# Three edits on three stages of a layered attention kernel: folded up-projections, one inversion for all causal sums, paired last chunks of a down product

## The reference

```python
# first stage, x after layernorm
q = (x @ Wq.T);  kv_latent = x @ Wkv_down.T           # 8 heads x 64; rank 64
k = kv_latent @ Wk_up.T;  v = kv_latent @ Wv_up.T      # 8 heads x 64
attn = softmax(q k^T * HEAD_DIM ** (-0.5));  x = x + (attn v) @ Wo.T
# feed-forward part of each of the four middle layers
a, g = split((layernorm(shift_token(x)) * lg + lb) @ w1 + b1)   # 682 each
x = x + (a * gelu(g)) @ w2 + b2
# causal stage, per head of 16
scores = dot * dot / (q_norm_sq + k_norm_sq.T - 2.0 * dot + EPSILON)   # masked above the diagonal
x = x + (softmax(scores) v) @ w_out + b_out
```

## Time and profile before

| | |
|---|---|
| median of 3 runs | 4794.3 us (4789.01 to 4796.3) |
| the profiled execution | 4790.7 us, span 4788.8 us |
| busy share of the span | PE 89%, PE weight loads 54%, DVE 70%, ACT 54%, POOL 33% |
| granted TensorE clock, mean | 0.947 |
| DMA | 77.63 MB, mean 16 GB/s |

### The profile page before, as it was taken

How to read it: one execution, slowest core, us unless ns; L and a number is a source line. 1 busy time by engine, 2 the same in 40 slices (tenths; PEclk the granted TensorE clock), 3 DMA queues, 4 the chain that set the end, 5 groups by cost and what they waited for, 6 DMA issues and landing times.

```text
span 4788.8 us, 65343 instructions
## 1 busy us (share of the span) xinstructions
PE 4268.6 (89%) x22880; PEld 2604.9 (54%) x22880; DVE 3362.2 (70%) x7872; ACT 2590.4 (54%) x5513; POOL 1586.9 (33%) x1816
## 2 busy tenths in 40 slices
PE   8989888999999999988788787777899999999997
PEld 4545455555555555655555555544555555555554
DVE  5555666676676676648999999998776666666662
ACT  4444444444444444427888988886444444444441
POOL 2121335454454454430000001012544454454441
PEclk9999999999999999997878888888999999999999
DMA  2000000000000000000000000011000000000000
GB/s 69 10 5 9 23 5 12 3 5 3 21 10 26 7 12 9 17 17 18 21 21 20 17 19 26 23 30 33 3 5 3 3 23 7 26 16 18 12 18 20
DMA packets 61206, 77.63 MB, mean 16 GB/s; under 512 B 13896, under 2 KB 45264, under 8 KB 60880
## 3 DMA queue, kind: packets, MB, share of 16 engines
q1 hardware_dynamic: 60880, 73.45, 5.3%
HBM read 35.70 MB, written 12.58 MB: 10 GB/s over the span
## 4 chain that ended last, share of the span: by engine, by line
PE 68%; DVE 20%; issue 5%; ACT 4%; POOL 2%; DMA 0%; SPq 0%; DVEq 0%; POOLq 0%; ACTq 0%
PE wide L762 50%; PE o_ps L762 8%; PE turn_ps L765 6%; PE wide L765 4%; DVE x L1179 3%; DVE w_up L1290 2%; DVE prob L1302 2%; DVE w_up L1275 2%; DVE x L1296 1%; POOL prob L1503 1%; DVE hid L1296 1%; DVE resid L1362 1%; DVE x L1394 1%; DVE k_t L1239 1%; ACT turned L1036 1%
## 5 line engine op out<-in xcount | busy, mean ns | idle before, releaser
L762 PE MATMUL wide<-x,w_up 128*128 128x512 f32 (+5 forms) x2432 | 872.9, 582 | 28.3 <-DVE x L1394 21.3
L762 PE MATMUL wide<-w_in,x_t 128*128 128x512 f32 (+1 forms) x1792 | 800.0, 589 | 56.6 <-ACT turned L1036 43.8
L1503 POOL TENSOR_SCALAR prob<-prob,st 128x256 f32<-128x256 f32 (+1 forms) x1024 | 444.3, 453 | 1036.0 <-DVE st L1326 1035.5
L1107 ACT ACTIVATE prob<-prob,st 128x256 f32<-128x256 f32 (+1 forms) x1024 | 479.4, 472 | 311.9 <-DVE st L1313 311.8
L762 PEld LDWEIGHTS wide<-w_in,x_t 128*128 128x128 f32 x1792 | 326.7, 192 | 406.3 <-issue 399.6
L762 PEld LDWEIGHTS wide<-x,w_up 128*128 128x128 f32 (+2 forms) x2432 | 353.2, 201 | 317.9 <-issue 282.9
L762 PE MATMUL o_ps<-pt,v 128*32 128x128 f32 (+2 forms) x5120 | 508.4, 345 | 15.8 <-DVE pt L1346 5.6
L765 PE MATMUL turn_ps<-ident,prob 128*128 128x128 f32 x2480 | 407.8, 283 | 73.3 <-issue 31.1
L1484 POOL TENSOR_TENSOR rn<-ss,minus_half 128x16 f32<-128x16 f32 x128 | 411.0, 3211 | 152.3 <-DVE ss L1225 145.2
L1476 POOL TENSOR_TENSOR sines<-raw,rot 128x512 f32<-128x512 f32 x256 | 350.6, 1390 | 320.6 <-ACT raw L1033 320.6
L765 PEld LDWEIGHTS turn_ps<-ident,prob 128*128 128x128 f32 x2480 | 285.2, 142 | 309.6 <-issue 249.8
(11 more groups left out here) (137 smaller groups left out, 7462.3 us busy)
## 6 DMA issues: line engine op xcount, KB each, us to landing
kept<-resid SPq DMA_DIRECT2D x16, 512.0 KB, 2.6
x<-kept SPq DMA_DIRECT2D x16, 512.0 KB, 3.3
w_up<-hid SPq DMA_DIRECT2D x64, 128.0 KB, 2.2
x<-hid SPq DMA_DIRECT2D x64, 128.0 KB, 2.4
shifted<-resid SPq DMA_DIRECT2D x32, 224.0 KB
w_in<-in_f_wqkv SPq DMA_DIRECT2D x4, 1536.0 KB, 6.8
w_up<-in_f_w SPq DMA_DIRECT2D x4, 1386.0 KB, 6.5
resid<-in_x SPq DMA_DIRECT2D x8, 512.0 KB, 8.0
```

What stands on the lines that cost most here:

```text
L762: return eng.matmul(out, lhsT, rhs, start=start, stop=stop, skip_group_check=True)
L1107: last = eng.activation(pr[:, local_span(t)], pr[:, local_span(t)], ACT.Exp, bias=sm[:, t:t + 1], scale=-1.0, accum_out=sm[:, 4 + t:5 + t])
L1503: last = eng.tensor_scalar(pr[:, local_span(t)], pr[:, local_span(t)], sm[:, 8 + t:9 + t], 1.0, ALU.mult, ALU.mult)
```

## The change

- First stage: `ak`, `av`, `lat_c` are gone. Two parts run once, ahead of everything: `fold_q` multiplies each head's query weights with its key up-projection (16 matmuls of 64 columns), and `fold_q_c` writes the product over `w_in`; `fold_o` multiplies each head's value up-projection with its output weights (8 matmuls of 256 columns) and `fold_o_c` writes `w_out`. Scores are taken against the latent, the mix runs over the latent too. `lat` makes the latent twice over, on rows 0 to 63 and 64 to 127 (weights of 128 columns), and once more with tokens on rows (8 matmuls of 64 columns); `ak_c` copies 512 columns and `av_c` 256. The weights for the folds are six DMAs ahead of the other sequences.
- Causal stage: `out` copies each group to `o_t`; once per unit `sel` gathers the sums of all 16 heads on 16 rows (4 accumulated matmuls), `olog` and `osum` invert them, and for each group `fan` spreads the inverses by a matmul of 16 rows, and `out_b` multiplies. `load_sel` loads both selection matrices into the room of `w_down`.
- Feed-forward: the last up-projection chunk is laid out so that tokens 0 to 255 have their values on rows 0 to 41 and tokens 256 to 511 on rows 64 to 105; `w_down`'s last rows are loaded on both; `down` goes over the token tiles 0, 2, 1, 3 and issues the 42-row matmuls of two tiles one after the other at the end of each second part. `gelu`'s last piece and `hid`'s are split in two by tokens.
- The table of costs: `lat` 2.9, `ak_c` 0.65, `av_c` 0.4, `sel` 2.55, `fan` 0.65, `osum` 1.2, `out_b` 0.65; feed-forward costs stay. The waits follow the new parts.

```diff
-UP = 2 * (HC - 1) * P + GATE_AT + HLAST
+WLAST = GATE_AT + HLAST
+UP = 2 * (HC - 1) * P + 2 * WLAST
...
+DOWN_TILES = [0, 2, 1, 3]
...
+LAST_ROWS = [slice(0, HLAST), slice(GATE_AT, WLAST)]
...
+    if st == "b":
+        put("sel", 0, u + 1, final("out", PAIRS - 1), ("load_sel", n * SEQS, 0))
+        put("olog", 0, u + 1, final("sel"), ("fan", u - 1, PAIRS - 1), ("nrm_f", u - 1, 0))
+        put("osum", 0, u + 1, final("olog"), ("down", u - 1, 3))
+        for g in range(PAIRS):
+            put("fan", g, u + 1, final("osum"))
+            put("out_b", g, u + 1, final("fan", g))
...
-                        at = 1024 + c * RANK
-                        last = mm(ps[0:RANK, 0:512], w_in[:, at:at + RANK], x_t[:, c, 1:1 + TOKENS],
-                                  c == 0, c == FC - 1)
+                        at = 1024 + c * 2 * RANK
+                        mm(ps[:, 0:512], w_in[:, at:at + 2 * RANK], x_t[:, c, 1:1 + TOKENS], c == 0, c == FC - 1)
+                    for t in range(TILES):
+                        for c in range(FC):
+                            at = 1024 + c * 2 * RANK
+                            last = mm(ps[:, 512 + t * RANK:512 + (t + 1) * RANK], x_t[:, c, 1 + t * P:1 + (t + 1) * P],
+                                      w_in[:, at:at + RANK], c == 0, c == FC - 1)
                     last.then_inc(S["lat"], 1)
-                elif kind == "ak":
-                    pe.wait_ge(S["lat_c"], nth("lat_c", u))
-                    for k in range(2):
-                        at = 1152 + (2 * i + k) * P
-                        last = mm(ps[:, k * 512:(k + 1) * 512], w_in[0:RANK, at:at + P], latent[0:RANK, :], True, True)
-                    last.then_inc(S["ak"], 1)
-                elif kind == "av":
-                    pe.wait_ge(S["lat_c"], nth("lat_c", u))
-                    for k in range(2):
-                        t = 2 * i + k
-                        last = mm(ps[:, k * 512:(k + 1) * 512], latent[0:RANK, t * P:(t + 1) * P],
-                                  w_in[0:RANK, 1664:2176], True, True)
-                    last.then_inc(S["av"], 1)
+                elif kind == "fold_q":
+                    pe.wait_ge(S["load_fold"], 16 * 6)
+                    for h in range(HEADS):
+                        for c in range(FC):
+                            at = c * INNER + h * HD
+                            last = mm(ps[:, at:at + RANK], fold_wq[h // 4][:, h % 4, c * P:(c + 1) * P], fold_wk[:, h, :],
+                                      True, True)
+                    last.then_inc(S["fold_q"], 1)
+                elif kind == "fold_o":
+                    pe.wait_ge(S["load_fold"], 16 * 6)
+                    for h in range(HEADS):
+                        r, at = 64 * (h % 2), h // 2 * DIM
+                        last = mm(ps[r:r + 64, at:at + DIM], fold_wv[:, h, :], fold_wo[h // 4][:, h % 4, :], True, True)
+                    last.then_inc(S["fold_o"], 1)
...
-                    pe.wait_ge(S["out"], nth("out", u, i))
-                    mm(turn_ps[:, :], sum_rows[:, :], o_raw, True, True).then_inc(S["sel"], 1)
+                    pe.wait_ge(S["out"], nth("out", u, PAIRS - 1))
+                    pe.wait_ge(S["load_sel"], 32)
+                    for g in range(GROUPS):
+                        last = mm(turn_ps[0:BHEADS, :], sum_rows[:, g, :], o_t[:, g, :], g == 0, g == GROUPS - 1)
+                    last.then_inc(S["sel"], 1)
+                elif kind == "fan":
+                    pe.wait_ge(S["osum"], 2 * nth("osum", u))
+                    mm(turn_ps[:, :], sum_fan[:, i, :], b_weight, True, True).then_inc(S["fan"], 1)
...
                     for k, m in enumerate((UP_G if kind == "up_g" else UP_H)[i]):
                         at, w = up_at(kind, m)
                         for c in range(FC):
-                            last = mm(ps[0:w, k * 512:(k + 1) * 512], w_up[:, c, at:at + w], x_t2[:, c, :],
-                                      c == 0, c == FC - 1)
+                            if m < HC - 1:
+                                last = mm(ps[:, k * 512:(k + 1) * 512], w_up[:, c, at:at + w], x_t2[:, c, :],
+                                          c == 0, c == FC - 1)
+                            else:
+                                for side in range(2):
+                                    cols = slice(256 * side, 256 * side + 256)
+                                    mm(ps[0:w, cols], w_up[:, c, at + side * w:at + (side + 1) * w], x_t2[:, c, cols],
+                                       c == 0 and side == 0, c == FC - 1)
                     last.then_inc(S[kind], 1)
                 elif kind == "down":
                     pe.wait_ge(S["hid"], nth("hid", u, HC // 2 - 1))
-                    pe.wait_ge(S["load_down"], 32 * f_count(n))
-                    for m in range(HC):
-                        w = P if m < HC - 1 else HLAST
-                        last = mm(ps[:, i * DIM:(i + 1) * DIM], hid[0:w, m, i * P:(i + 1) * P], w_down[0:w, m, :],
-                                  m == 0, m == HC - 1)
+                    pe.wait_ge(S["load_down"], 48 * f_count(n))
+                    t = DOWN_TILES[i]
+                    for m in range(HC - 1):
+                        last = mm(ps[:, t * DIM:(t + 1) * DIM], hid[:, m, t * P:(t + 1) * P], w_down[:, m, :], m == 0, False)
+                    if i % 2:
+                        for t in DOWN_TILES[i - 1:i + 1]:
+                            last = mm(ps[:, t * DIM:(t + 1) * DIM], hid[LAST_ROWS[t // 2], HC - 1, t * P:(t + 1) * P],
+                                      w_down[LAST_ROWS[t // 2], HC - 1, :], False, True)
                     last.then_inc(S["down"], 1)
...
-                elif kind == "lat_c":
+                elif kind == "av_c":
                     act.wait_ge(S["lat"], o)
-                    act.wait_ge(S["ak"], nth("ak", u - 1, 1))
-                    act.wait_ge(S["av"], nth("av", u - 1, 1))
-                    eng.activation(latent[0:RANK, :], wide[PLACE["lat", u, 0]][0:RANK, 0:512], ACT.Copy
-                                   ).then_inc(S["lat_c"], 1)
-                elif kind == "av_c":
-                    act.wait_ge(S["av"], o)
                     att_done(act, u - 2)
-                    eng.activation(v[s][:, 2 * i:2 * i + 2, :].rearrange("p t n -> p (t n)"),
-                                   wide[PLACE["av", u, i]][:, :], ACT.Copy).then_inc(S["av_c"], 1)
+                    eng.activation(v[s][:, 0, 0:TILES * RANK], wide[PLACE["lat", u, 0]][:, 512:512 + TILES * RANK], ACT.Copy
+                                   ).then_inc(S["av_c"], 1)
+                elif kind == "fold_q_c":
+                    act.wait_ge(S["fold_q"], 1)
+                    eng.activation(w_in[:, 0:FC * INNER], wide[PLACE["fold_q", u, 0]][:, :], ACT.Copy
+                                   ).then_inc(S["fold_q_c"], 1)
...
                     eng.activation(hid[:, 0:HC - 1, :], hid[:, 0:HC - 1, :], ACT.Gelu)
-                    rows = slice(GATE_AT, GATE_AT + HLAST)
+                    ps = wide[PLACE["up_h", u, 0]]
                     act.wait_ge(S["up_h"], nth("up_h", u, 0))
                     act.wait_ge(S["down"], nth("down", u - 1, TILES - 1))
-                    eng.activation(hid[0:HLAST, HC - 1, :], wide[PLACE["up_h", u, 0]][rows, 0:512], ACT.Gelu,
-                                   bias=bias_up[rows, 2 * HC - 1:2 * HC]).then_inc(S["gelu"], 1)
+                    for side in range(2):
+                        to, of, cols = LAST_ROWS[side], LAST_ROWS[1 - side], slice(256 * side, 256 * side + 256)
+                        last = eng.activation(hid[to, HC - 1, cols], ps[of, cols], ACT.Gelu, bias=bias_up[of, 2 * HC - 1:2 * HC])
+                    last.then_inc(S["gelu"], 1)
...
+                elif kind == "osum":
+                    dve.wait_ge(S["oexp"], o)
+                    dve.wait_ge(S["down"], nth("down", u - 1, TILES - 1))
+                    eng.tensor_tensor(o_rest, turn_ps[0:BHEADS, :], b_weight, ALU.mult).then_inc(S["osum"], 1)
+                    dve.wait_ge(S["osum"], 2 * o - 1)
+                    eng.scalar_tensor_tensor(out=b_weight, in0=o_rest, scalar=2.0, in1=b_weight, op0=ALU.subtract,
+                                             op1=ALU.mult).then_inc(S["osum"], 1)
                 elif kind == "out_b":
-                    dve.wait_ge(S["oexp"], o)
-                    dve.wait_ge(S["proj"], nth("proj", u - 1, TILES - 1))
-                    eng.tensor_tensor(o_t[:, i, :], turn_ps[:, :], b_weight, ALU.mult).then_inc(S["osum"], 1)
-                    dve.wait_ge(S["osum"], 2 * o - 1)
-                    eng.scalar_tensor_tensor(out=b_weight, in0=o_t[:, i, :], scalar=2.0, in1=b_weight, op0=ALU.subtract,
-                                             op1=ALU.mult).then_inc(S["osum"], 1)
-                    dve.wait_ge(S["osum"], 2 * o)
-                    eng.scalar_tensor_tensor(out=o_t[:, i, :], in0=o_raw, scalar=-1.0, in1=b_weight, op0=ALU.mult,
```

(31 more changed lines are left out.)

183 lines of the change are left out of this document (85 added, 98 removed).

## The result

The changed kernel takes 4719.6 us (median of 4 runs, 4717.2 to 4734.7) against 4794.7 (4 runs, 4789.0 to 4796.3): 0.985 of before, 95% interval 0.9839 to 0.9862. It is faster by 75 us where 110 were forecast: inside the range of 4645 to 4735, above the band of 4655 to 4703 that was given 0.60, and just at the 4720 of rival C. Its profiled execution is 4717.2 us, span 4715.3.

The account below looks back on a forecast made before the run. PE was taken to bound the first stage and feed-forward units, DVE the causal stage. Gains of 36 + 2 + 48 + 24 = 110 us took the profiled 4790.7 to 4681, median 4684 us, range 4645 to 4735.

Parts of the forecast that it names:

- rival C: First stage gives nothing: steps at the 7.77 us floor everywhere and a lower clock; 4720 us, chance 0.10.
- Feed-forward: 32 units: pairing the 42-row `down` matmuls saves 1.64 us per unit, 1.5 net, 48 us in all, bounds 22 to 55.
- Rival A: Feed-forward: the two 42-row matmuls don't run together, so it gives 25 us; 4707 us, chance 0.11.
- First stage: 8 units: PE's net saving of 5.9 us per unit leaves 4.5, 36 us in all, bounds 8 to 52.
- With fewer fillers about one more step falls to the floor: I give back 1.0: First stage: 1.0 us per unit of PE's 5.9 saved is lost to idle time at the 7.77 us step floor.
- The 0.4 for the clock: First stage: 0.4 us per unit lost because a PE with more pauses is oftener at 1.2 GHz.
- The prediction's own sign, first-stage units above 79: The forecast called itself wrong if first-stage units stayed above 79 us; it expected them near 76.7.
- The start: Before the first score: 2 us of gain, range -5 to +5, first score at 28 to 36 us against 32.41.
- I take 0.11: Price in us of each 64-column record past 128 weight columns, from transposes; `fold_q`'s 32 records came to 3.5 us.
- Causal stage: 8 units: DVE 4.1 us less, about a quarter of PE's added 5 counted; 3 per unit, 24 in all, -8 to 36.
- about a quarter: Causal stage: the share of PE's added 5 us per unit that counts, its share of the chain; 1.1 us.
- rival D: Causal stage: the line behind the last mix overruns its slack, 15 us exposed per unit; 4828 us, chance 0.03.

Follow-up runs that it names:

- x3: Changed kernel with the 42-row `down` matmuls of two tiles adjacent, but all on rows 0 to 41: 4753.6 us, 0.9927 of the kernel before.
- x2: Changed kernel with the `down` edit undone, one 42-row matmul ending each tile, GELU and `hid` in one piece: 4779.2 us, 0.9975 of before.
- x7: Changed kernel with first-stage `proj`, four query parts, `lat` and `xt` put between transposes of the narrow tile: 4691.1 us, 0.9799 of before.
- x10: As x7, but `mix` is also cut in two halves and fillers stand in seven of a unit's eight steps: 4657.3 us, 0.973 of before.
- x6: Changed kernel with first-stage row maxima over 256 of the 512 columns of each half: 4726.1 us, 0.9869 of before.
- x8: Changed kernel with each `fan` matmul of the causal stage issued twice: 4778.9 us, 0.9978 of before.
- x9: Changed kernel with `fold_q` waiting only for its own loads and heads 4 to 7 on rows 64 to 127: 4720.4 us, 0.9862 of before.
- x1: Changed kernel with the first-stage folding undone (`ak`, `av`, `lat_c` and old loads back): 4724.2 us, 0.9861 of before.
- x12: Kernel before with the causal edit alone, fold and paired `down` undone: 4778.0 us, 0.9977 of before.
- x5: Changed kernel with first-stage copies out of the narrow tile moving 256 of 512 columns, so its result is not the layer's: 4685.0 us, 0.9781 of before.
- x11: x10 and x9's start together, against the kernel before: 4656.5 us, 0.9729.

## Why the prediction was right or wrong

The time lies in the stated range, 35 us above the forecast. By the two profiled executions 31 us of that are the first stage and the start (6.9 in place of 38), 7 the causal stage (17.2 in place of 24), and the feed-forward units gave 1.5 more than forecast.

- **Feed-forward: right**, 48 us: 1.5 a unit, made of a turn (x3) and the running together (x2), each at its forecast size. Rival A is out.
- **First stage: wrong.** The step that failed is "With fewer fillers about one more step falls to the floor: I give back 1.0". PE's work fell as computed, 5.9; given back were 4.1. The mistake was to take room as a property of the step ("an unfilled step holds some 1.6 us of idle") and the floor as that of the chain over the wide buffers. The 1.6 is right in size (0.83 + 0.69), but the room is two holes at fixed places, and taking out a filler that stands in one is worth 0.76 less than its length. The four removed parts stood in holes: 4 x 0.76 = 3.0 of the 4.1. The rest goes with the wait of 1.29 us behind the second score, which stands in each of the first five units after and in none before. The orders of x7 and x10 don't have it either, but no run changed it alone.
  The 0.4 for the clock was too small as well. Over the first five distances between `proj`, six traces with the fold and the same order (after, x2, x3, x6, x8, x9) have 81.7 us in the mean, 2.3 above their 79.4 at full clock; three without it (before, x1, x12) 82.2, 1.1 above their 81.1. So slow stretches took another 1.2 a unit, and of the 4.5 forecast some 0.5 was left in the mean (1.0 from before to after, and 2.0 and 0.0 in the last two distances). By the seven distances from the first `proj` to the eighth the folded runs (584 to 595 us) and the unfolded ones (588 to 595) overlap. So rival C, put at 0.10, had the cause half right (idle time and the clock, though not every step stood at 7.77) and its 4720 was the time, partly by chance: the causal edit came out lower too. The prediction's own sign, first-stage units above 79, came true.
- **The start: wrong in sign**, +5.4 against -2, both ends by x9: 2.6 us of waiting for the output weights, which was foreseen, and `fold_q` at 0.21 us a record, where "I take 0.11" had been from 128-row transposes. The 128-row, 64-column records of `lat` do come at that pitch (16 in 1.73 us, from 27.75 to 29.48). The load rows of `fold_q`, 64 rows in one row group, have 0.33 us in the mean against 0.14 for the transposes; the 64-row loads of the scores have 0.20, so few rows alone don't explain it, and what does wasn't tried.
The Trainium skill, "TensorE: Matmul & The Clock Gate", section "LDWEIGHTS (loading the stationary operand)", has a load's time by its columns alone, however few rows; by it the 32 loads would take 32 x 0.107 = 3.4 us, an estimate. On one row group this trace disagrees as to what the records cost, with 7.0. The 3.6 us of x9 come near 3.4, but not by shorter loads: its records are still 0.21 apart, in pairs. The Trainium skill, "TensorEngine Tiling (Array Packing)", section "Key Properties", says that different tiles can load and multiply in parallel; x9's two groups agree, with 3.6 us in place of 7.0.
- **Causal stage:** inside it right (2.8 a unit against 3), with a wrong split: PE's part was priced at "about a quarter", where x8 has on this line 7.4 us a unit for 5.4 added. DVE's waits behind `fan` and the new inversion came to 30.8 us, 3.9 a unit, above the 3 set as the mark of an error. Before, the inversion cost it 11.5; the 2.4 a unit more would account for 4.9 us less work on DVE giving 2.8, which is argued and not tried. The edges, 4.2 us in x12, were not in the sum. That rival D's line behind the last mix shows in them is likely but not shown; 15 us exposed in every unit it is not.

## What to carry to other kernels

Ask of each piece of work on the bounding engine not only how long it is but which wait it covers: removing 1.91 us that covered 0.76 is worth 1.15 here. A floor is identified by shortening one link at a time (x5, x6), and a single-buffered tile between two engines costs a round trip at each use unless other work is written into it: x10 gained 62 us by order and by cutting parts smaller, some 10 of them PE's time at the lower clock. In an order computed by a planner, look where the shorter work has been put.

## What was not expected of the hardware

- On one group of 64 rows, records of 64 columns came 0.21 us apart (7.0 for 32); on two groups they came in pairs at the same distance, 3.6 us for 32.
- In x5, x10 and x11 PE kept the higher of its two clock levels over the first five first-stage units (1.00), in after and x7 three of the five have a stretch at the lower level that costs up to 3.4 us, and in x2 all five. Less idle time alone doesn't decide it: x7 has 7.1 us a unit and x5, in shorter pauses, 8.6. What does decide it wasn't tried.
